# A fused two-layer adapter network on one Trainium2 core: down-adapter ranks taken by token half, left-over features merged with the adapter's second factor

## The reference

```python
def lora_add(base, inp, A, B):           # A, B chosen per batch by lora_indices
    t = einsum('bri,bni->bnr', A[idx], inp)
    return base + einsum('bor,bnr->bno', B[idx], t) * 0.5
gate = lora_add(x @ W_gate.T, x, A_gate, B_gate)      # 1024 -> 2752
up   = lora_add(x @ W_up.T, x, A_up, B_up)
act  = silu(gate) * up
down = lora_add(act @ W_down.T, act, A_down, B_down)  # 2752 -> 1024
out  = x + down @ sign(weight).T + bias
```

## Time and profile before

| | |
|---|---|
| runs | 2056.28, 2058.56, 2059.4 us; median 2058.56 |
| profiled execution | 2058.98 us |
| its span | 2057.3 us, 33381 instructions |
| mean granted TensorE clock | 0.991 |
| TensorE / VectorE / ScalarE / GpSimd busy | 98% / 72% / 36% / 25% |
| matmuls | 9320 |
| DMA | 217.84 MB, mean 106 GB/s |

### The profile page before, as it was taken

One profiled execution on the slowest core, in us unless ns is written; L12 is line 12 of the kernel. 1 busy time (PEld: TensorE's weight loads), 2 busy tenths in 40 slices (PEclk: granted clock), 3 DMA queues, 4 the chain that ended last, 5 costly groups with the idle time before them and its releaser, 6 DMA issues. The chain is left out here.

```text
span 2057.3 us, 33381 instructions
## 1 busy us (share of the span) xinstructions
PE 2010.0 (98%) x9320; PEld 1672.9 (81%) x9320; DVE 1476.3 (72%) x2424; ACT 744.1 (36%) x1394; POOL 518.5 (25%) x900
## 2 busy tenths in 40 slices
PE   6999999999999999999998999999999999999998
PEld 5878888888887888888897788888889778888886
DVE  6578777776758777777666777777756777777774
ACT  3234333332333333333334433333323443333330
POOL 6132222213212222221502222222160232222100
PEclk8999999999999999999999999999999999999999
DMA  9265554542435555554243854444424565544401
GB/s 241 91 134 115 114 114 103 114 99 59 106 88 126 113 114 114 114 114 89 55 130 73 161 111 105 105 104 103 97 62 128 112 137 114 113 103 105 94 21 41
DMA packets 311092, 217.84 MB, mean 106 GB/s; under 512 B 167801, under 2 KB 301817, under 8 KB 311009
## 3 DMA queue, kind: packets, MB, share of 16 engines
q1 hardware_dynamic: 274528, 188.62, 40.1%
q0 software_dynamic: 35328, 24.03, 6.7%
q10 hardware_dynamic: 1152, 4.19, 0.5%
HBM read 203.89 MB, written 12.58 MB: 105 GB/s over the span
## 5 line engine op out<-in xcount | busy, mean ns | idle before, releaser
L1166 PE MATMUL ps<-x,split 128*128 128x512 f32 x1440 | 566.0, 393 | 14.5 <-DVE split L744 10.4
L1168 PE MATMUL ps<-x,split 128*128 128x512 f32 x1440 | 563.0, 391 | 0.0
L1167 PE MATMUL ps<-x,split 128*128 128x512 f32 x1440 | 562.3, 391 | 0.0
L541 ACT ACTIVATE split<-ps 128x512 fp32r<-128x512 f32 x368 | 218.7, 599 | 486.8 <-DVE ps L758 474.2
L1166 PEld LDWEIGHTS ps<-x,split 128*128 128x128 f32 x1440 | 272.1, 189 | 70.2 <-issue 12.2
L446 POOL DMA_DIRECT2D nat_ad<-L_cond_A_down x224 | 137.0, 618 | 724.9 <-DVE ps L758 714.2
L1168 PEld LDWEIGHTS ps<-x,split 128*128 128x128 f32 x1440 | 271.6, 189 | 58.9
L1167 PEld LDWEIGHTS ps<-x,split 128*128 128x128 f32 x1440 | 271.6, 189 | 57.2
L952 DVE TENSOR_TENSOR acc<-ps,acc 128x512 f32<-128x512 f32 x252 | 173.1, 689 | 143.3 <-PE ps L1168 143.3
L1166 PE MATMUL ps<-hidden 128*128 128x512 f32 (+1 forms) x704 | 273.9, 389 | 0.0
L1168 PE MATMUL ps<-hidden 128*128 128x512 f32 (+1 forms) x704 | 273.8, 389 | 0.0
(11 more groups left out here) (110 smaller groups left out, 2679.0 us busy)
## 6 DMA issues: line engine op xcount, KB each, us to landing
nat<-L_cond_W_gate SPq DMA_DIRECT2D x336, 128.0 KB
nat<-L_cond_W_up SPq DMA_DIRECT2D x336, 128.0 KB
nat_down<-L_cond_W_down SPq DMA_DIRECT2D x112, 384.0 KB
nat_a<-L_ffn_weight SPq DMA_DIRECT2D x96, 128.0 KB, 2.7
nat<-effective_weight SPq DMA_DIRECT2D x24, 512.0 KB
nat<-x SPq DMA_DIRECT2D x16, 512.0 KB
nat_b<-L_cond_B_gate POOLq DMA_DIRECT2D x224, 24.0 KB, 2.5
nat_b<-L_cond_B_up POOLq DMA_DIRECT2D x224, 24.0 KB, 2.5
```

The source lines that it names most:

```text
L541: act.activation(dst, src, func).then_inc(piece_hi, 1)
L1166: pe.matmul(dst, a[0], b[0], start=first, stop=False)
L1167: pe.matmul(dst, a[0], b[1], start=False, stop=False)
L1168: return pe.matmul(dst, a[1], b[0], start=False, stop=last)
```

## The change

1. **Left-over features of down.** `down_rest` is gone from TensorE, with its nine copies. The left-over activation is written to a new tensor `rest_in` (high and low), each token half in 64 partitions; the other 64 partitions of that half take the ranks of the down adapter later. The rows DREM of W_down are turned at the end of the last part instead of in the head, and share their `split` slots with the second factor BD: token half 0 uses a slot with BD in partitions 0 to 63 and DREM in 64 to 127, half 1 the reverse. The final product (`last_products`) has 2 halves x 3 matmuls of 256 columns.
2. **Ranks by token half.** The 128 rank rows of a half are 64 rows by the high and 64 by the low weights, and its 512 columns 256 by the high and 256 by the low activation: 3 matmuls a half and part, 6 a part, in two outputs (rows 9 and 10 of `acc`). `ranks_rest` adds the left-over features' share in the last part, one matmul a half. At the end VectorE adds the column halves (`down_columns`), ScalarE copies one partition half across, VectorE adds, masks, and both split (`down_ranks`).
3. **First part copied.** Part 0 is written out ahead of the inner loop, which now runs 5 times; its `down_add` is a copy (`down_first`).
4. **Head order.** On VectorE and ScalarE: rank 0, G0, rank 1, U0, ADREM, S6, S7, left-over activation, G1. On TensorE the left-over rows' adapter product comes between G0's weights and U0's; U0 no longer waits for the left-over activation, G1 does.
5. **Loads and memory.** SP loads the first W_down part before the sign rows of the head; the left-over rows (now into all four partition quadrants) at the group's end. GpSimd loads the left-over rows of A_down twice (into both partition halves). `out_sb` now lies over a part of the activations, so ScalarE and VectorE wait for the stored output before they write there.

```diff
-HEAD = (["B"] * 3 + ["AG"] * 2 + ["AU"] * 2 + ["REM"] * 2 + ["BREM"] + ["DREM"] * 2 + ["ADREM"]
-        + ["G0"] * 2 + ["U0"] * 2 + ["S6"] * 2 + ["S7"] * 2 + ["G1"] * 2)
+HEAD = (["B"] * 3 + ["AG"] * 2 + ["AU"] * 2 + ["REM"] * 2 + ["BREM"] + ["G0"] * 2 + ["U0"] * 2
+        + ["ADREM"] + ["S6"] * 2 + ["S7"] * 2 + ["G1"] * 2)
-LAST = PART[:13] + ["BD"] * 2
+LAST = PART[:13] + ["BD"] * 2 + ["DREM"] * 2
-DOWN_ORDER = (8, 0, 1, 2, 3, 4, 5, 6, 7)
+STAGE = 2 + KC
+DOWNS = STAGE * NQ
+DOWN_BANKS = (3, 4, 5, 3, 4, 5, 3, 4, 5, 3)
+LAST_BANKS = (3, 4, 5, 0, 1, 2, 3, 4, 5, 3)
...
+            def down_columns(g):
+                dve.wait_ge(down_added, ADDED + DOWNS * (g + 1) - KC)
+                dve.wait_ge(act_lo, START + ACTS * (g + 1))
+                dve.tensor_tensor(act_f[:].rearrange("p (h t) -> p h t", h=2), acc[:, KC:, 0:256], acc[:, KC:, 256:512],
+                                  ALU.add).then_inc(ranks_added, 1)
+            def down_ranks(g):
+                dve.wait_ge(ranks_moved, g + 1)
+                for rows, tokens in HALVES:
+                    last = dve.tensor_tensor(act_f[rows, tokens], act_f[rows, tokens], gated[rows, tokens], ALU.add)
+                last.then_inc(ranks_whole, 1)
+                dve.wait_ge(ranks_whole, g + 1)
...
+                dve.wait_ge(rank_hi, 3 * g + 3)
+                for rows, tokens in HALVES:
+                    last = lo(rest_in[rows, 1, tokens], act_f[rows, tokens], rest_in[rows, 0, tokens])
+                last.then_inc(rank_lo, 1)
...
                 if last:
-                    b_down_unit(g, q, SPLIT_BD)
+                    b_down_unit(g, q)
                     act_tile(g, q, 2)
-                    down_add(g, q + 1, 0)
-                    rank(g, 2)
-                    for i in range(1, 9):
-                        down_add(g, q + 1, i)
-                        if i == 5:
+                    down_rest(g, q)
+                    for i in range(2):
+                        down_add_last(g, i)
+                    down_columns(g)
+                    last_lows(g, q, "DREM", lambda half: 1 - half)
+                    down_ranks(g)
+                    for i in range(2, STAGE):
+                        down_add_last(g, i)
+                        if i == 6:
                             down_low(g, 0)
...
                 rank(g, 0)
-                down_rest(g)
-                a_down_rest(g)
-                rank(g, 1)
                 weight_unit(g, 0, "G0", NAT_FIRST[0], SPLIT_GU)
+                rank(g, 1)
                 weight_unit(g, 0, "U0", NAT_FIRST[1], SPLIT_GU + 1)
-                act_rest(g)
-                for i in range(9):
-                    down_add(g, 0, i)
+                a_down_rest(g)
                 sign_unit(g, 0)
                 sign_unit(g, 1)
+                act_rest(g)
+                dve.wait_ge(out_stored[0], 64 * (START + g))
                 weight_unit(g, 0, "G1", NAT_FIRST[2], SPLIT_GU + 2)
-                with dve.Fori(0, NQ - 1) as q:
+                part(g, 0, False, lambda g, q, i: down_first(g, i))
+                with dve.Fori(1, NQ - 1) as q:
...
+                def ranks(half, js, stop):
+                    tokens = HALVES[half][1]
+                    for j in js:
+                        mm = pe.matmul(ps[:, rank_banks[half], :].rearrange("p (s t) -> p s t", s=2),
+                                       lora_ad[:, j, 2 * half:2 * half + 2, :].rearrange("p b r -> p (b r)"),
+                                       acts[:, :, j, tokens], start=(j == 0), stop=(stop and j == PT - 1))
+                    return mm
+                def last_products(i):
+                    for half, (_, tokens) in enumerate(HALVES):
+                        mm = product(ps[:, banks[i], tokens], stationary(SPLIT_BD + half, i - 2),
+                                     [rest_in[:, s, tokens] for s in range(2)], False, half == 1)
+                    mm.then_inc(down_psum, 1)
...
+                for half in range(2):
+                    ranks(half, (0, 1), False)
+                tiles(2, (0, 1))
+                pe.wait_ge(act_lo, START + ACTS * g + PT * q + 4)
+                for half in range(2):
+                    ranks(half, (2,), False)
+                    ranks_rest(half).then_inc(down_psum, 1)
+                tiles(2, (2,), False)
+                pe.wait_ge(up_read, START + ACTS * (g + 1))
+                for i in (3, 4, 5):
+                    tiles(i, range(PT), False)
                 pe.wait_ge(piece_lo, START + LOW_PIECES * (g + 1))
                 pe.wait_ge(rank_lo, START + 3 * g + 3)
-                for i in (1, 2, 3):
-                    adapter(i)
+                for i in (2, 3, 4, 5):
+                    last_products(i)
```

More of the change, by code:

```diff
@@ L378, in _ @@
                 group(g)
-                for p in range(4):
+                for p in range(3):
                     load_x(g + 1, p, g)
+                load_down_rest(g)
+                load_x(g + 1, 3, g)
                 load_weight(g + 1, 0)
@@ L617, in act_tile, with last_weights @@
                 copy(acts[:, 0, j, :], act_f[:]).then_inc(act_hi, 1)
+            def last_weights(g, q, name, slot_of):
+                c = first_of(name)
+                for half in range(2):
+                    cols = slice(512 * half, 512 * half + 512)
+                    act.wait_ge(piece_turned, piece_number(g, q, c + half) + 1)
+                    for i, (rows, _) in enumerate(HALVES):
+                        last = copy(split[rows, slot_of(i), 0, cols], bank_of(c + half)[rows])
+                    last.then_inc(piece_hi, 1)
             def part(g, q, last):
@@ L628, in part @@
                 c = first_of("AD")
-                piece(g, q, c, lora_ad[:, 0].rearrange("p j a -> p (j a)"), bank_of(c)[:, 0:PT * P])
+                piece(g, q, c, lora_ad[:, :, 0::3, :],
+                      bank_of(c)[:, 0:PT * P].rearrange("p (j h r) -> p j h r", j=PT, h=2))
                 if last:
-                    unit(g, q, "BD", SPLIT_BD - PART_UNITS * q)
+                    for m in (SPLIT_BD, SPLIT_BD + 1):
+                        slot_read(g, q, m - PART_UNITS * q)
+                    last_weights(g, q, "BD", lambda half: half)
                     act_tile(g, q, 2)
+                    last_weights(g, q, "DREM", lambda half: 1 - half)
                     return
@@ L795, in adapter_unit, with last_lows, b_down_unit @@
                 unit_lows(g, 0, c, m)
-            def b_down_unit(g, q, m):
+            def last_lows(g, q, name, slot_of):
+                c = first_of(name)
+                for half in range(2):
+                    cols = slice(512 * half, 512 * half + 512)
+                    dve.wait_ge(piece_hi, piece_number(g, q, c + half) + 1)
+                    for i, (rows, _) in enumerate(HALVES):
+                        last = lo(split[rows, slot_of(i), 1, cols], bank_of(c + half)[rows],
+                                  split[rows, slot_of(i), 0, cols])
+                    last.then_inc(piece_lo, 1)
+            def b_down_unit(g, q):
                 dve.wait_ge(nat_a_full[0], 128 * (2 * g + 2))
@@ L810, in b_down_unit @@
                     t.then_inc(piece_turned, 1)
-                unit_lows(g, q, c, m)
+                last_lows(g, q, "BD", lambda half: half)
             def sign_unit(g, i):
@@ L956, in down_low, with part @@
                 lo(down(1, m), acc[:, m, :], down(0, m)).then_inc(down_lo, 1)
-            def part(g, q, last):
+            def part(g, q, last, add=down_add):
                 weight_unit(g, q, "U1", NAT_GU + 3, SPLIT_GU + 3)
@@ L1286, in tiles, with ranks_rest @@
+                def ranks_rest(half):
+                    rows, tokens = HALVES[1 - half][0], HALVES[half][1]
+                    return pe.matmul(ps[:, rank_banks[half], :].rearrange("p (s t) -> p s t", s=2),
+                                     ad_rest[rows].rearrange("p b r -> p (b r)"), rest_in[rows, :, tokens],
+                                     start=False, stop=True)
                 def tiles(i, js, stop=True):
-                    m = DOWN_ORDER[i]
+                    m = i - 2 if last else i
```

256 lines of the change are left out of this document (139 added, 117 removed).

## The result

The changed kernel takes **2011.72 us** (median of 4 runs, 2011.21 to 2012.24), the kernel before 2058.64 (4 runs): ratio **0.9774**, 95% interval 0.9762 to 0.9786. Forecast: 2017.0, range 2005 to 2032. The profiled execution took 2011.54 us, with a span of 2009.8 against 2057.3.

What follows compares the result with a forecast made beforehand. TensorE, 98% busy, was taken to bound the kernel, with VectorE's chain setting the heads. Heads 39.0 plus middle parts 16.4 less last parts 13.6 took 41.8 us off the 2057.3 span: 2015.5, so 2017 us; range 2005 to 2032.

Steps and rivals of the forecast that it cites:

- Matmuls removed: TensorE, each group: 46 matmuls fewer at 0.2274 us; 10.2 us a group saved, 40.7 over four, with waits unchanged.
- rival D: Second factor's 176 matmuls: half-and-half moving operand read at half pace, 40 us lost, 2057, no change; chance 0.03.
- Middle parts: Six middle parts a group: three matmuls less each, 0.68 us a part, 16.4 us saved in all.
- Heads: Start of the four groups: VectorE's chain sets nextG0's start, earlier by 10.1, 10.1, 10.1 and 8.7 us; 39.0 saved.
- Moved loads. All at nothing: Left-over W_down rows, big W_down load ahead of the signs, GpSimd's eight more small loads a group: no cost or gain.
- Last phase: Last part of each group: less cover for VectorE's chains, 3.4 us a group lost, 13.6 in all; bounds 0 and 6.
- Costs the same whether its contraction is 128 or 64 rows deep: TensorE's pace: 512-column products of either depth take 388 to 390 ns each, overlapped.
- The clock's 0.5: Last part, wait before rest_in: a quarter to a third of a 1.8 us half-pace loss, counted as 0.5 us.
- A: Last part: rank chain takes 4 us more than summed, TensorE waits 6 us and returns at 1.2 GHz; 2038; chance 0.14.
- B: Waits covered: last parts lose nothing and the heads' G1 comes 0.5 earlier; 2001; chance 0.08.
- C: Inner loop jumps: instruction fetch costs TensorE 3.69 us at each of 20, 74 us, 90 with clock; 2105; chance 0.03.

Runs made afterwards that it cites:

- e5: Changed kernel with the three rank products of one token half issued twice in each of the six parts that are not the last; 2026.80 us, ratio 0.9852.
- e1: Changed kernel with nine additions of 128x512 added on VectorE in the head, ahead of weight unit G1; 2036.58 us, ratio 0.9894.
- e2: Changed kernel with U0's 24 products with x1 issued twice on TensorE in each head, nothing added on VectorE; 2021.44 us, ratio 0.9826.
- e9: Changed kernel with SP's first W_down load put back behind the sign rows and the head's third gate/up load; 2047.90 us, ratio 0.9955.
- e10: Changed kernel with the left-over activation put back before the two sign units on VectorE and ScalarE; 2020.30 us, ratio 0.9819.
- e3: Changed kernel with the two 64-row products of ad_rest issued first in the last down phase; 2015.59 us, ratio 0.9793.
- e4: Changed kernel with one output tile of the last down phase moved ahead of the wait for rest_in; 2007.73 us, ratio 0.9754.
- e7: Changed kernel with the 64-row products first in the last down phase and one output tile ahead of the wait for the ranks; 2002.80 us, ratio 0.9728.
- e6: Changed kernel with VectorE's loop over the groups written out as three copies of the body; 2005.82 us, ratio 0.9743.

## Why the prediction was right, and where it was not

- **Matmuls removed** (46 a group, 0.2274 us): right. 9232 matmuls; the rank products last 395 ns, so rival D (half pace) is out.
- **Middle parts**, -16.4: measured -16.3; e5 puts it back.
- **Heads**, -39.0: measured -41.4. G1's waits were 0.22, 2.81, 2.58 and 0.27 us (forecast 3.4 in two, below 1 in the others), nextG0's 0.75, 0.76, none in group three, where the half clock behind G1's wait makes TensorE late, 0.71 (forecast 1.2 to 1.5). That VectorE's chain sets the head is shown by e1 and e2. The chain came out shorter than summed: U1's transposes begin in group two at 623.69, 22.3 us after the rank multiply (601.35) where I had 22.8. The clock fell in group three, as I had it for both, and not in group two; either way nextG0 hid most of it.
- **"Moved loads. All at nothing"**: this step was wrong, and by it the total was right partly by luck. Of the heads' 41.4 us, 36.7 hang on the moved W_down load; with it in its old place the copies are gone and the heads are 1.4, 0.5, 1.9 and 0.9 us shorter than before. My sum let VectorE's chain move 10 us ahead and asked of SP only whether it had time. What had to be asked is when U1's rows are ready if VectorE no longer holds their load back. The 0.79 us in the earlier trace rows do not answer it, since that load was issued behind the copies; the queue does. In e9 the rows are ready 40.0 us after the head's start. The kernel before had them at 41.4 and wanted them at 40.6; the chain without the copies wants them at 31.0, hence the wait of 9.0 and a head only 1.4 us shorter than before. The right price of the move was "nothing lost, and 36 kept". Both parts are needed: e1 gives VectorE 5.5 us of its work back and loses 24.9. The kernel before with the load alone moved was not run.
- **Head order**: I gave the new order no term of its own. e10 shows 8.6 us in the place of the left-over activation; the other moves of the order (G0 before rank 1) have no run.
- **Last phase**, +13.6: measured +11.5, by other terms. Wait for the third activation: 0.83 from the starts (forecast 0.7). Before `rest_in`: forecast 9.9 of chain less 7.7 of matmuls = 2.2; measured 9.65 from 481.56 to 491.21 less 8.65, which is 1.0. The matmuls took 0.9 longer where 64-row and 128-row products alternate. "Costs the same whether its contraction is 128 or 64 rows deep" held for the rows that I read, where the products of one size follow each other, and not here; the 0.9 lay under the chain and so cost nothing. The clock's 0.5 did not come. I had placed the wait between one of 3.54 with a fall and one of 1.50 without; but the kernel before has one of 1.57 at 125.22, and its clock is 0.50 from 126 to 128. e3, with a wait of 1.92, nearly the one I had forecast, shows the loss in three groups of four.
- **Rivals**: A (chain 4 us longer) had the right place; the chain was 0.25 shorter. B (covered) is what e4 and e7 make, at -4.0 and -8.9. C (a jump's cost at the inner loops) did not appear; the outer jump's 3.4 us is real, by e6.

## What to carry over

When an edit moves a chain ahead, ask of each load that it uses what holds its issue and what stands ahead of it in its queue. A small wait on a load may only mean that the load is held back by the chain itself; how late it would be without the hold is read from the landing of the transfers ahead of it. Price an edit in front of a wait with the chain that ends the wait: it may buy nothing, or, through the clock, less than nothing, and turn to gain once something covers the wait. Extra work on one engine at a time (nine additions, 24 matmuls) tells cheaply whose chain a stretch is.

## What the runs showed of the hardware

- TensorE with alternating 128-row and 64-row operands takes 0.43 us a 512-column step, against 0.227. Its weight loads in the changed kernel:

```profile
481.99 0.18 PEld L1389 LDWEIGHTS ps<-rest_in,ad_rest 64*128 64x128 f32 x1 [0.25 <-issue]
482.41 0.19 PEld L1381 LDWEIGHTS ps<-hidden,lora_ad 128*128 128x128 f32 x1 [0.24 <-issue]
...
483.62 0.19 PEld L1260 LDWEIGHTS ps<-hidden 128*128 128x128 f32 x1
483.85 0.19 PEld L1258 LDWEIGHTS ps<-hidden 128*128 128x128 f32 x1
```

  At each change the load starts only with its own matmul (0.25 us of standing first); with equal rows loads follow each other at the matmuls' pace, hidden. The Trainium skill, "TensorE: Matmul & The Clock Gate", section "The mechanism", says that a weight load overlaps with running matmuls only when the row groups differ, and names loads to a background weight buffer as another that is pulled ahead. This trace differs from the first: loads of the same 128 rows are hidden, and those where the number of rows changes are not; which buffer a load goes to no run shows. In e3, with the two 64-row products side by side, the two changes cost 0.19 us together.
- The clock fell to 0.50 for some 3.5 us after waits of TensorE of 1.57 us (before, first head), 1.92 (e3, last down phase), 2.58 (changed kernel, third head) and 2.82 (e3, second head); it stayed at 1.00 after 1.90 (e3, group four) and 2.81 (changed kernel, second head). The length of the gap alone does not tell.
- A wait of TensorE costs about 0.27 us more than the profile lists, where the clock does not fall.
